# A graph layer and an expert layer on one core: all experts for eight node groups computed while edge rows are gathered, rows kept in DRAM, one-hot as stationary operand

## The chip, the cores and the metric

The kernel runs on one core of a Trainium2 chip. The metric is the device time of one launch in microseconds (us), the median of several runs.

## What is computed

12500 nodes have a row of 256 float32 each. There are two residual blocks, a graph layer and a mixture of experts:

```
x = x + segment_sum((layernorm(x) @ W)[src] * edge_weight[:, None], dst) + b      # 200000 edges
y = layernorm(x)
logits = mean(y, nodes) @ Wr + br            # one routing for all nodes
two experts of 8 are chosen, with weights r0 and r1
h_e = gelu(y @ W1[e] + b1[e]);  z_e = h_e @ W2[e] + b2[e]                          # 256 -> 512 -> 256
x = x + layernorm(y + r0 * z_e0 + r1 * z_e1) * gamma + beta
```

The edges come sorted by destination. The destination is `12500 * u**2` with uniform `u`, so that low nodes have far more edges than high ones: the first 128 nodes have about 158 blocks of 128 edges, the last 128 about 8. The routing depends on the mean over all nodes, so which two experts are needed is known only after the last node's first block is done.

## The kernel before

Nodes are cut into 98 tiles of 128 (`NT`), edges into 1563 blocks of 128 (`NE`). A small program (`Queue.put`, `Queue.run`) keeps a list of instructions for each engine, written in the order in which the source calls `put`; an instruction waits on the semaphores of its `after` list.

**Gather phase.** POOL (`gather`, L380) issues one indirect DMA for each edge block: 128 rows of `x` of 1 KB into `G`, a ring of 32 buffers. VectorE (DVE) takes the statistics of the gathered rows (`variance`, L395, `variance_end`, L401), works out the reciprocal roots for 8 blocks at a time (`power`, L412 to L427, written in between the other work), and builds a one-hot matrix scaled by weight and root (`one_hot`, L436, ring of 8). TensorE (PE) multiplies in `edge_tile` (L480): for each half of 128 columns of the block, `G` is the stationary operand and the one-hot moves, which adds to a 256 x 128 transposed sum in `ps` bank 0. Tiles are walked from node 0 up. When a tile's edges are through, `end_tile` adds the tile's column sum (L469), multiplies the sum by `W` (L473) and adds `b` (L474), then L487 begins the next tile with the edge block that straddles the border. ScalarE (ACT) takes the sum out (`node_tile`, L533), builds the one-hot of the straddling block, adds x, and computes mean and root (L543 to L560). All tiles of the new x stay in SBUF in `X`, 98 KB in each partition. All 12.8 MB of x are loaded into it by 25 DMAs at the start.

**Routing** is a chain of small instructions on PE, DVE and ACT (L624 to L665), then the two chosen experts are loaded and split in a high and a low part (L687, L688).

**Expert phase.** 25 groups of 4 tiles. `turn` (L591) transposes a normalised group on PE; `up` (L712) does 48 matmuls of 512 columns, `down` (L732) 96 of 256 columns, both in the high and low parts (three products), one pass of PE each. ACT computes the gelu twice (L716, L718), DVE the low part (`Hlo`, L721). The sum, the statistics and the normalisation of the group before are put between (`sum_up` L739 to L742, `rstd` L746 and L747, `finish` L752 to L757 with gamma and beta on POOL, `give` L763 and the store), as are `norm2` (L584), `rest_of_y` (L605) and `add_bias` (L611, POOL).

```
def edge_tile(r, gathered):
    ...
    for c in range(2):
        ins = e.matmul(ps[:, 0, c * P:(c + 1) * P], G[:, r, c * P:(c + 1) * P], OH[:, r % OHR, :], start=False, stop=True, skip_group_check=True)
    ins.then_inc(s_main.handle, 1)
    with e.While(lambda: e.snap(nxt) == e.snap(edge)):
        end_tile()
```

Of the kernel before, what the change touches and what calls it, by code (L numbers as in the profile page):

```python
# [12 lines left out]
HID = 2 * F // P  # L13
RING, OHR, NB = 32, 8, 8
# [3 lines left out]

class Sem:

    def __init__(self, handle):
        self.handle, self.value = handle, 0

class Queue:

    def __init__(self, new_sem):
        self.new_sem, self.sems, self.lists = new_sem, {}, {}  # L30

    def sem(self, name):
        if name not in self.sems:
            self.sems[name] = Sem(self.new_sem(name))
        return self.sems[name]

    def put(self, engine, fn, after=(), inc=None, by=1):
        s = self.sem(inc) if inc else None
        self.lists.setdefault(engine, []).append((fn, tuple(after), s, by))
        if s is None:  # L40
            return None
        s.value += by
        return (s, s.value)

    def run(self, engine, eng):
        reached = {}
        for fn, after, s, by in self.lists.get(engine, []):
            for w, v in after:
                if reached.get(w, 0) < v:
                    eng.wait_ge(w.handle, v)  # L50
                    reached[w] = v
            ins = fn(eng)
            if s is not None:
                ins.then_inc(s.handle, by)

def gnn_ffn(nc, x, dflat, srct, dstt, wt, W, b, Wr, br, W1, b1t, W2, b2, gamma, beta, cst, iota_e, out):
# [6 lines left out]

    srct_s, dstt_s, wt_s = dram("srct_s", (P, NE), i32), dram("dstt_s", (P, NE), i32), dram("wt_s", (P, NE))

    ctx = ExitStack()
    with ctx:
        def sb(name, shape, dt=f32):
            return ctx.enter_context(nc.sbuf_tensor(name, shape, dt))  # L70

        ctx.enter_context(nc.allow_non_contiguous_dma(reason="an expert's biases, an edge's columns"))
        q = Queue(lambda name: ctx.enter_context(nc.semaphore(name)))
        put = q.put

        X = sb("X", [P, NT, D])
# [5 lines left out]
        eps, half3, mhalf = sb("eps", [P, 1]), sb("half3", [P, 1]), sb("mhalf", [P, 4])  # L83
# [4 lines left out]

        base = (nc.sbuf_base + 31) // 32 * 32  # L90
        ARENA = 24576
        sb("arena", [P, ARENA + 8])

        class At:
# [778 lines left out]
```

## Time and profile before

| | us |
|---|---|
| median of 3 runs (2610.92 to 2613.72) | 2611.01 |
| span of the profiled execution | 2609.0 |
| first gather issued, last gather issued | 11.1, 1972.4 |
| last edge block on PE | 1985.1 |
| first matmul of the expert phase | 2006.4 |
| mean granted TensorE clock, share of full | 0.807 |

The span runs from the first instruction of an execution to its last. Engines run side by side and wait for each other by semaphores, so a share of busy time tells little by itself: the table shows two phases after each other, and each has to be read by what its own waits end on. The profiled execution's own time is its span and the few microseconds around it: 2609.0 against a median of 2611.0.

### The profile page before, as it was taken

What the parts mean: (1) busy time and instruction counts of PE and PEld (TensorE: products, weight loads), DVE (VectorE), ACT (ScalarE), POOL (GpSimd) and SP (SyncE); (2) the same over time, 40 slices, a digit from 0 to 9 for tenths busy, and PEclk for the clock granted to TensorE, in tenths of its full rate; (3) what the DMA queues carried; (4) which work ended last, traced back from release to release, by engine and by line L of the source; (5) the groups of instructions that cost most, each with busy time, mean ns of one, the idle gap of its engine ahead of it and who ended that gap; (6) DMA issues with size and microseconds to landing.
All of it is one profiled execution on the core that took longest, in us unless ns stands there. A gap on an engine that the chain in (4) does not pass through costs nothing.

```text
span 2609.0 us, 43640 instructions
## 1 busy us (share of the span) xinstructions
PE 2236.6 (86%) x11252; PEld 1768.6 (68%) x11253; DVE 1934.6 (74%) x8411; ACT 809.6 (31%) x2323; POOL 1725.3 (66%) x1665
## 2 busy tenths in 40 slices
PE   4799988888888888878788888888888999999998
PEld 3576666666666665665566655565666888888887
DVE  6777777777777777777777777777786666666666
ACT  0001000011121222223333344444456445444543
POOL 6777777777777777777777777777772343344344
PEclk9755566666667677778877898889898999999999
DMA  7633333333333333333333333333332000000000
GB/s 252 205 105 105 105 105 105 105 105 105 105 105 105 105 105 105 105 105 105 105 105 105 105 105 105 105 105 105 104 105 67 17 23 19 25 25 17 25 25 28
DMA packets 104845, 239.16 MB, mean 92 GB/s; under 512 B 26637, under 2 KB 53430, under 8 KB 104696
## 3 DMA queue, kind: packets, MB, share of 16 engines
q0 software_dynamic: 75024, 204.97, 26.9%
q1 hardware_dynamic: 29240, 30.25, 3.6%
q10 hardware_dynamic: 432, 2.40, 0.3%
q8 instruction: 40, 0.66, 0.1%
q14 instruction: 109, 0.89, 0.1%
HBM read 224.71 MB, written 12.80 MB: 91 GB/s over the span
## 4 chain that ended last, share of the span: by engine, by line
PE 43%; DMA 18%; POOL 17%; DVE 12%; issue 9%; ACT 1%; ACTq 0%; DVEq 0%; POOLq 0%
PE ps L480 19%; DMA G<-in_x,SRC 17%; POOL G L380 14%; PE ps L712 7%; PE ps L473 5%; PE ps L732 5%; PE ps L474 2%; PE ps L469 2%; DVE ST L395 2%; PE ps L487 2%; DVE OH L436 2%; POOL Z L755 1%; DVE Z L763 1%; DVE YTl L605 1%; DVE Hlo L721 1%
## 5 line engine op out<-in xcount | busy, mean ns | idle before, releaser
L380 POOL DMA_INDIRECT G<-in_x,SRC x1563 | 1486.4, 951 | 486.5 <-issue 292.5
L480 PE MATMUL ps<-OH,G 128*128 128x128 f32 x6252 | 1283.4, 356 | 310.1 <-DVE OH L436 292.6
L480 PEld LDWEIGHTS ps<-OH,G 128*128 128x128 f32 x6252 | 1041.2, 244 | 540.2 <-DVE OH L436 528.8
L395 DVE BATCH_NORM_STATS2 ST<-G 128x6 f32<-128x256 f32 x1563 | 666.6, 426 | 410.1 <-DMA G<-in_x,SRC 380.6
L436 DVE TENSOR_SCALAR OH<-CST,DL,WR 128x128 f32<-128x128 f32 x1563 | 530.8, 340 | 0.0
L533 ACT ACTIVATE AT<-ps 128x256 f32<-128x256 f32 x98 | 37.5, 383 | 1119.8 <-PE ps L480 1119.6
L401 DVE BATCH_NORM_AGGREGATE MV<-ST 128x2 f32<-128x6 f32 x1563 | 296.9, 190 | 6.8
L716 ACT ACTIVATE Ht<-ps,b1s 128x512 f32<-128x512 f32 (+1 forms) x200 | 136.4, 682 | 309.7 <-PE ps L712 292.4
L732 PE MATMUL ps<-W2h,Hhi 128*128 128x256 f32 x784 | 224.1, 286 | 0.4 <-DVE Hlo L721 0.4
L732 PE MATMUL ps<-W2l,Hhi 128*128 128x256 f32 x784 | 222.0, 283 | 0.0
L732 PE MATMUL ps<-W2h,Hlo 128*128 128x256 f32 x784 | 221.9, 283 | 0.0
L747 POOL TENSOR_TENSOR ZR<-ZR,mhalf 128x4 f32<-128x4 f32 (+1 forms) x25 | 26.3, 1053 | 290.2 <-DVE ZR L746 290.1
L721 DVE TENSOR_TENSOR Hlo<-Ht,Hhi 128x512 fp32r<-128x512 f32 (+1 forms) x200 | 129.7, 681 | 78.7 <-ACT Hhi L718 78.5
L763 DVE SCALAR_TENSOR_TENSOR Z<-X,NM,Z 128x256 f32<-128x256 f32 x98 | 89.1, 967 | 110.8 <-POOL Z L757 110.7
L473 PE MATMUL ps<-Wsb,AT 128*128 128x256 f32 x392 | 154.3, 532 | 3.2 <-ACT AT L533 1.9
L732 PEld LDWEIGHTS ps<-W2h,Hhi 128*128 128x128 f32 x784 | 150.5, 192 | 0.8 <-DVE Hlo L721 0.6
L732 PEld LDWEIGHTS ps<-W2l,Hhi 128*128 128x128 f32 x784 | 150.6, 192 | 0.0
L732 PEld LDWEIGHTS ps<-W2h,Hlo 128*128 128x128 f32 x784 | 150.5, 192 | 0.0
L473 PEld LDWEIGHTS ps<-Wsb,AT 128*128 128x128 f32 x392 | 92.5, 262 | 84.3 <-issue 72.6
L712 PE MATMUL ps<-YTh,W1h 128*128 128x512 f32 (+1 forms) x400 | 124.6, 393 | 13.5 <-DVE YTl L605 13.5
L718 ACT ACTIVATE Hhi<-ps,b1s 128x512 fp32r<-128x512 f32 (+1 forms) x200 | 135.1, 676 | 0.0
L755 POOL TENSOR_TENSOR Z<-Z,g_bc 128x1024 f32<-128x1024 f32 x24 | 95.3, 3973 | 58.2 <-DVE Z L752 58.2
(141 smaller groups left out, 2290.2 us busy)
## 6 DMA issues: line engine op xcount, KB each, us to landing
G<-in_x,SRC POOLq DMA_INDIRECT x1563, 2.7
X<-in_x SPq DMA_DIRECT2D x24, 512.0 KB
out<-Z SPq DMA_DIRECT2D x24, 512.0 KB, 3.0
W1s<-in_W SPq DMA_DIRECT2D x2, 512.0 KB, 4.4
W2s<-in_W SPq DMA_DIRECT2D x2, 512.0 KB, 6.1
DF<-in_dflat SPq DMA_DIRECT2D x1, 782.0 KB, 6.5
DST<-in_dstt ACTq DMA_DIRECT2D x1, 781.5 KB, 6.3
SRC<-in_srct ACTq DMA_DIRECT2D x1, 781.5 KB, 8.6
```

The lines of the kernel that those rows point to most:

```text
L380: gathered[s] = put("pool", lambda e: e.indirect_dma_start(out=G[:, s % RING, :], out_offset=None, in_=x, in_offset=bass.IndirectOffsetOnA ...
L395: bn[s] = put("dve", lambda e: e.bn_stats(ST[:, s % 4, :], G[:, s % RING, :]), after=[gathered[s]] + ([aggr[s - 4]] if s >= 4 else []), in ...
L401: aggr[s] = put("dve", lambda e: e.bn_aggr(MV[:, b_ % 2, k, :], ST[:, s % 4, :]), after=[bn[s]] + ([scaled[b_ - 2]] if b_ >= 2 else []), i ...
L436: oh[s] = put("dve", lambda e: e.tensor_scalar(OH[:, s % OHR, :], iota, DL[:, s:s + 1], WR[:, s + 1:s + 2], ALU.is_equal, ALU.mult), after ...
L473: e.matmul(ps[:, 1, 0:D], AT[:, c * P:(c + 1) * P], Wsb[:, c, :], start=False, stop=True, skip_group_check=True)
L480: ins = e.matmul(ps[:, 0, c * P:(c + 1) * P], G[:, r, c * P:(c + 1) * P], OH[:, r % OHR, :], start=False, stop=True, skip_group_check=True)
L712: hid[(g, i)] = put("pe", lambda e, c=c, k=k, f=f, bank=bank, wp=wp, yp=yp, st=(wp is W1h and yp is YTh and c == 0), en=(wp is W1l and c = ...
L716: h = put("act", lambda e, i=i, bank=bank, b1c=b1c: e.activation(Ht[:, i % HB, 0:n], ps[:, bank, 0:n], ACT.Gelu, bias=b1c), after=[hid[(g, ...
L718: h = put("act", lambda e, i=i, bank=bank, b1c=b1c: e.activation(Hhi[:, i, 0:n], ps[:, bank, 0:n], ACT.Gelu, bias=b1c), after=[w1_ok[1]] + ...
L721: hlo[(g, i)] = put("dve", lambda e, i=i: e.tensor_tensor(out=Hlo[:, i, 0:n], in0=Ht[:, i % HB, 0:n], in1=Hhi[:, i, 0:n].bitcast(f32), op= ...
L732: l2[(g, i)] = put("pe", lambda e, j=j, rows=rows, i=i, k=k, f=f, hp=hp, wp=wp, st=(i == 0 and j % 2 == 0 and hp is Hhi and wp is W2h), en ...
L755: gm = put(engine, lambda e: e.tensor_tensor(out=Z[:, g % 2, 0:n, :], in0=Z[:, g % 2, 0:n, :], in1=g_bc[:, :].unsqueeze(1).to_broadcast([P ...
```

## The change

The kernel is written anew as one program for each engine, with explicit waits. What it does otherwise:

- **Edges.** Edges and tiles are walked from the last node down. The one-hot is the stationary operand and `G` moves with 256 columns: one float32 product instead of two. The sum comes out as nodes x 256, so that a tile's end (a *section*) first transposes it. `G` has 64 buffers, `OH` 10; a gather waits for PE (`s_main`) and also for the statistics 32 blocks back (`s_bn`).
- **Sections** (`chores`) are spread over later ones: copy, transpose, product with `W` and `b`, x added, roots of a group of 4 tiles at a time, normalised rows transposed. Results go to DRAM: `x1_d` (the new x), `yt_d` (its normalised transpose). x is loaded tile by tile.
- **Units.** For the first 8 groups walked (`AHEAD`; the 32 tiles with the highest nodes), each of the 8 experts is computed in plain float32 while the gather goes on: 64 units. An up half is 8 products of 512 columns and four gelus, a down half 16 products of 256 columns and two copies; each unit loads 512 KB of `W1` and of `W2` and stores 512 KB to `y_d`. `events()` lists when each half is due; PE reads the due edge from a table (`EVT`) and branches.
- **After the routing** only 17 groups go through `up` and `down`. For the other 8 the two chosen experts' results are read back from `y_d`; they are put between the others (`order`, `pre_of`). Groups are not turned on PE, but read back transposed. POOL adds the second biases and `beta` (`add_rows`), DVE does all of the rest.

```diff
-RING, OHR, NB = 32, 8, 8
+RING, GS, OHR = 64, 32, 10
+AHEAD = 8
+UNITS = AHEAD * E
...
+def events():
+    free, u, out = 0.0, 0, []
+    for t in range(NT):
+        lo, hi = (min(NT - 1 - t + k, NODES / P) / (NODES / P) for k in range(2))
+        free += NE * (hi ** 0.5 - lo ** 0.5) * 0.8 - 2.9 if t >= 11 else 0.0
+        n = max(0, min(int(free / 14.2), UNITS - u))
+        n = UNITS - u if t == NT - 1 else n
+        free -= 14.2 * n
+        mine = [(round(64 * (k + 1) / (2 * n + 1)) / 64, kind, u + k // 2) for k, kind in enumerate([UPS, DOWNS] * n)]
...
-            for c in range(2):
-                ins = e.matmul(ps[:, 0, c * P:(c + 1) * P], G[:, r, c * P:(c + 1) * P], OH[:, r % OHR, :], start=False, stop=True, skip_group_check=True)
+            def edge(a, r):
+                g = e.snap(((a + r) & (RING - 1)) * D)
+                e.wait_ge(s_oh, a + (r + 1))
+                e.matmul(ps[:, 0, 0:D], OH[:, r, :], Gf[:, bass.ds(g, D)], start=False, stop=True, skip_group_check=True).then_inc(s_main, 1)
...
+            for s in range(NE):
+                if s >= RING:
+                    e.wait_ge(s_main, s - RING + 2)
+                if s >= GS:
+                    e.wait_ge(s_bn, s - GS + 1)
+                e.indirect_dma_start(out=G[:, s % RING, :], out_offset=None, in_=x,
...
+            def chores(v):
+                e.wait_ge(s_as, v + 1)
+                e.wait_ge(s_at, v + 1)
+                for c in range(2):
+                    ins = e.transpose(ps[:, TA, c * P:(c + 1) * P], AS[:, c * P:(c + 1) * P], ident)
+                ins.then_inc(s_ta, 1)
+                e.wait_ge(s_pre, v + 1)
+                for c in range(2):
+                    e.matmul(ps[:, XB, 0:D], AT[:, c * P:(c + 1) * P], Wsb[:, c, :], start=False, stop=True, skip_group_check=True)
+                e.matmul(ps[:, XB, 0:D], ones[0:1, :], b_row[0:1, :], start=False, stop=True, skip_group_check=True).then_inc(s_w, 1)
...
+            def unit_up(u):
+                e.wait_ge(w1_in, u * 16 + 16)
...
+                for i in range(4):
+                    e.wait_ge(s_gelu, u4 + (i + 1))
+                    for c in range(2):
+                        ins = e.matmul(ps[:, UP[i % 2], :], W1u[:, c, i * P:(i + 1) * P], YU[:, c, :], start=(c == 0), stop=(c == 1))
+                    ins.then_inc(s_up, 1)
...
+            def unit_down(u):
...
+                for p in range(2):
+                    e.wait_ge(s_ye, u * 2 + (p + 1))
+                    for h in range(2):
+                        j = 3 - (2 * p + h)
+                        for i in range(4):
+                            ins = e.matmul(ps[:, DN[p], h * D:(h + 1) * D], H[:, i, j * P:(j + 1) * P], W2u[:, i, :],
+                                           start=(h == 0 and i == 0), stop=(i == 3), skip_group_check=True)
+                    ins.then_inc(s_dn, 1)
...
+            with e.Fori(0, NE // OHR) as i:
+                a = e.snap(i * OHR)
+                e.reg_mov(rel, e.snap(due) - a)
+                for half in (range(0, OHR // 2), range(OHR // 2, OHR)):
+                    with e.If(e.snap(rel) > half[-1]):
+                        for r in half:
+                            edge(a, r)
+                    with e.If(e.snap(rel) <= half[-1]):
+                        for r in half:
+                            event(a, r, edge(a, r))
...
+                    else:
+                        e.wait_ge(yp_in[g % 2], 32 * (g // 2 + 1))
+                        e.scalar_tensor_tensor(out=Z[:, n % 2, q, :], in0=YP[:, g % 2, 0, q, :], scalar=r1[:, 13:14], in1=XN[:, n % 3, q, :], op0=ALU.mult, op1=ALU.add).then_inc(s_zy, 1)
...
+                        e.scalar_tensor_tensor(out=Z[:, n % 2, q, :], in0=YP[:, g % 2, 1, q, :], scalar=r1[:, 14:15], in1=Z[:, n % 2, q, :], op0=ALU.mult, op1=ALU.add).then_inc(s_z, 1)
```

## Rows read from the trace of the kernel before

**Rows 1.** The page's first lines: span, then busy time and share of each engine.

```profile
span 2609.0 us, 43640 instructions
PE 2236.6 (86%) x11252; PEld 1768.6 (68%) x11253; DVE 1934.6 (74%) x8411; ACT 809.6 (31%) x2323; POOL 1725.3 (66%) x1665
```

**Rows 2.** Stretches: window, length, busy us (instructions), granted clock, DMA share, GB/s.

```profile
60.00:100.00 40.00, 27.87 (x130) 23.37 (x128) 29.32 (x153) 0.00 (x0) 30.43 (x32) 0.74 0.76 231
200.00:400.00 200.00, 178.09 (x675) 136.57 (x674) 155.75 (x759) 17.43 (x58) 151.42 (x160) 0.60 0.36 105
1600.00:1900.00 300.00, 250.77 (x1274) 181.98 (x1272) 232.25 (x1136) 140.00 (x494) 227.18 (x240) 0.86 0.36 105
2300.00:2600.00 300.00, 290.41 (x1902) 265.17 (x1900) 199.48 (x450) 137.31 (x230) 123.35 (x51) 1.00 0.07 22
```

**Rows 3.** Instructions in order of time: POOL's gathers without and with a wait.

```profile
12.58 0.95 POOL L380 DMA_INDIRECT G<-in_x,SRC  x1 [0.30 <-issue]
...
1972.41 0.94 POOL L380 DMA_INDIRECT G<-in_x,SRC  x1 [0.30 <-PE ps L480]
```

**Rows 4.** Waits: us in total, times, longest.

```profile
DVE ST L395 <- DMA G<-in_x,SRC: 380.6, 1141, 2.2
...
PEld ps L487 <- issue: 38.9, 97, 0.7
```

**Rows 5.** In order of time, PE: a tile's end and the burst after it.

```profile
692.54 0.79 PE L469 MATMUL ps<-X,RCOL 128*1 x2
693.25 1.13 PE L473 MATMUL ps<-Wsb,AT 128*128 128x256 f32 x4
694.32 0.69 PE L474 MATMUL ps<-b_row,ones 1*128 1x256 f32 x2
694.94 0.71 PE L487 MATMUL ps<-OHX,G 128*128 x4
...
1952.01 4.35 PE L480 MATMUL ps<-OH,G 128*128 128x128 f32 x32
```

**Rows 6.** The chain that ended last, two groups of the expert phase: start, us, what.

```profile
2019.48 11.54 PE ps L732 x96
2031.02 10.91 PE ps L712 x48
...
2296.51 11.15 PE ps L712 x48
...
2320.68 11.15 PE ps L712 x48
```

**Rows 7.** PE alone in two windows; columns as in Rows 2 without the other engines.

```profile
304.00:308.00 4.00, 3.55 (x13) 0.50 0.37 108
320.00:324.00 4.00, 4.00 (x24) 0.89 0.36 102
```

**Rows 8.** Around the routing, in order of time.

```profile
1985.13 0.52 PEld L480 LDWEIGHTS ps<-OH,G 128*128 128x128 f32 x4 [0.18 <-issue]
...
1992.49 1.28 ACT L623 ACT_TABLE_LOAD   x1
...
2006.41 1.20 PE L712 MATMUL ps<-YTh,W1h 128*128 128x512 f32 x2
```

**Rows 9.** DMA issues: KB each, median us from issue to landing.

```profile
W1s<-in_W SPq DMA_DIRECT2D x2, 512.0 KB, 4.4
```

**Rows 10.** Groups of instructions (busy us, mean ns) in the window from 2200 to 2500 us.

```profile
L716 ACT ACTIVATE Ht<-ps,b1s 128x512 f32<-128x512 f32 x103 | 71.1, 690 | 169.6 <-PE ps L712 161.1
...
L741 DVE BATCH_NORM_STATS2 ZST<-Z 128x6 f32<-128x256 f32 x52 | 22.2, 428 | 1.8
...
L584 DVE TENSOR_SCALAR Y<-X,R 128x256 f32<-128x256 f32 x52 | 14.8, 349 | 0.0
```

**Rows 11.** Single lines: durations in ns, min/median/max, of all of the span.

```profile
L763 DVE SCALAR_TENSOR_TENSOR Z<-X,NM,Z x98: 471/474/2628, 2049.8 to 2604.7; 128x256 f32<-128x256 f32 x98
L611 POOLq MODIFY_POOL_CONFIG  x2: 33/35/37, 1973.3 to 1973.4; - x2
```

More of the change, by code:

```diff
@@ L12 @@
 NC = (NE + P - 1) // P
-HID = 2 * F // P
-RING, OHR, NB = 32, 8, 8
+RING, GS, OHR = 64, 32, 10
+SHIFT = (NT - 1) * P
 LN_EPS = 1e-5
 CAPACITY = float(-(-NODES * 5 // (4 * E)))
[L19 to L54, printed above, removed]
@@ L57, in gnn_ffn, with tiles, slot, sections @@
-def gnn_ffn(nc, x, dflat, srct, dstt, wt, W, b, Wr, br, W1, b1t, W2, b2, gamma, beta, cst, iota_e, out):
+GT = 4
+NG = (NT + GT - 1) // GT
+AHEAD = 8
+UNITS = AHEAD * E
+HID = 2 * F // P
+HB = 4
+VIRTUAL = 4
+FINAL = NT - 1 + VIRTUAL
+END, EXTRA, UPS, DOWNS = range(4)
+def tiles(g):
+    return range(g * GT, min((g + 1) * GT, NT))
+def slot(t):
+    return len(tiles(t // GT)) - 1 - t % GT
+def sections():
+    copied = [v if v < NT - 1 else NT - 1 if v == FINAL else None for v in range(FINAL + 5)]
+    out, waiting, turned = [], [], None
+    for v in range(FINAL + 5):
+        x1 = copied[v - 2] if v >= 2 else None
+        root = x1 // GT if x1 is not None and (x1 == NT - 1 or x1 % GT == GT - 1) else None
+        waiting += tiles(root) if root is not None else []
+        xh = waiting.pop(0) if waiting else None
+        out.append({"copy": copied[v], "across": copied[v - 1] if v else None, "x1": x1, "root": root, "xh": xh, "yt": turned})
+        turned = xh
+    assert not waiting and turned is None
+    return out
@@ L190, in gnn_ffn @@
[L190 to L198 removed]
+        OHX, OHT = early("OHX", [P, P]), early("OHT", [P, 2, P])
@@ L726, in down @@
-        def down(g):
-            for i in range(HID):
-                k, f = i // 4, i % 4
-                for j, t in enumerate(tiles(g)):
-                    rows = slice(j * P, (j + 1) * P)
-                    for hp, wp in ((Hhi, W2h), (Hhi, W2l), (Hlo, W2h)):
-                        l2[(g, i)] = put("pe", lambda e, j=j, rows=rows, i=i, k=k, f=f, hp=hp, wp=wp, st=(i == 0 and j % 2 == 0 and hp is Hhi and wp is W2h), en=(i == HID - 1 and hp is Hlo): e.matmul(
-                            ps[:, j // 2, j % 2 * D:(j % 2 + 1) * D], hp[:, i, rows], wp[:, k, f, :], start=st, stop=en, skip_group_check=True),
-                            after=[hlo[(g, i)], w2_ok[k]] + ([z[(g - 1, j // 2 * 2 + 1)]] if g else []), inc="pe_down")
-                    l2[(g, "end", j)] = l2[(g, i)]
@@ L843 @@
+            up(0)
+            for k in range(len(post)):
+                down(k)
+                if k + 1 < len(post):
+                    up(k + 1)
 def kernel(**inputs):
@@ L859 @@
     cst[0, 5 * P + E] = 1 << 20
+    evt = np.zeros((NT + 1, 2 * NEV), np.float32)
+    for n, (t, c, kind, _) in enumerate(EVENTS):
+        evt[t, 2 * n] = 1 - c
+        evt[t + 1, 2 * n] = c if t + 1 < NT else c * (NE - 1)
+        evt[NT, 2 * n + 1] = kind
+    evt[NT, 2 * NEV - 2] = 1 << 20
     arrays = {
```

1422 lines of the change are left out of this document (877 added, 545 removed).

## The prediction

> **What bounds the kernel now.** The busy table comes first [rows 1]: TensorE 86%, DVE 74%, POOL 66%, none of them full. Cut into stretches [rows 2] it falls into two phases. Between 200 and 400 us POOL starts 160 gathers, 1.25 us each, and it does the same in every stretch until its last one; from 2300 on it does something else. In order of time [rows 3] the first gathers, which wait for nothing, and the last, which wait for PE, show the same picture: about 0.95 us of work and 0.30 us until the next. (1972.41 - 12.58) / 1561 gathers is 1.255 us. So in the gather phase nobody but POOL sets the pace: PE and DVE wait for it, DVE 380.6 us for the gathers' data [rows 4]. That PE is 89% busy from 200 to 400 us [rows 2] is no contradiction. Its granted clock is 0.60 there: PE was let run mostly at 1.2 GHz, because what it has to do fills a slow PE and would leave a fast one half empty. In the burst after a late tile's end 32 matmuls of 128 columns take 4.35 us at full clock [rows 5], 0.136 each, four to an edge block: 0.54 us of work in 1.255.
>
> In the expert phase the chain of what ended last [rows 6] is made of PE's `up` and `down`: 11.15 and 11.54 us, and one group takes 2320.68 - 2296.51 = 24.17 us. PE is 97% busy at full clock there [rows 2]. The kernel is thus 1974 us of POOL, 32 us of tail and routing, 603 us of PE. The change moves PE work out of the third part into the idle half of PE in the first.
>
> **PE's prices in the new gather phase.** From [rows 6], one-pass matmuls of 512 columns cost 10.91 / 48 = 0.227 us, of 256 columns 11.54 / 96 = 0.120: 0.42 ns a column and pass and 13 ns an instruction. A float32 product runs as two instructions (L480's x32 in [rows 5] are 8 blocks of 2 products), each of two passes. So 256 columns cost 2 x (512 x 0.42 + 13) = 0.456 us, 512 columns 0.886. The tile's end gives the upper bound: L473's two products of 256 columns take 1.07 us from start to start, 0.535 each, with a gap in it [rows 5]. I take 0.47 for 256 columns, near the steady stream, and 0.89 for 512.
>
> - Edge: 0.47 us (0.456 to 0.535), against 0.54 now.
> - Section: from L469's start to the next burst is 695.49 - 692.54 = 2.95 us now (L487 starts at 694.94, 0.55 before the burst) [rows 5]. L469 goes (0.71), four transposes come (4 x 0.13 by the burst's price, 0.5), the rest stays: 2.75, with two waits for ACT that aren't in it now. I take 2.9, bounds 2.75 and 3.8 (one further idle 0.4 us as before each L487, 38.9 / 97 [rows 4], at each of its two transposes).
> - Unit: 8 x 0.89 + 16 x 0.47 = 14.6 us (14.4 to 16).
>
> By the destination's density the first 11 tiles take 87 blocks; until then no unit is scheduled and PE follows POOL: 11 + 87 x 1.255 + 10 for DVE's lead = 130 us. What follows is 1476 x 0.47 = 694, 91 sections x 2.9 = 264, 64 units x 14.6 = 934: 1892 us, and PE is through at 130 + 1892 = 2022. POOL alone would let it finish where it does now, at 1985 [rows 8]. **So the new bound of the gather phase is PE, not POOL, by a small margin**, and the last edge moves by +37 us. Both ends: 1985 (edge 0.456, section 2.75, unit 14.4 give 1976, less than POOL) and 130 + 1476 x 0.535 + 91 x 3.8 + 64 x 16 = 2290. Of the clock: the level stayed at 1.2 GHz in a window in which PE waited for a one-hot now and then, and 2.4 GHz came in one in which it had fallen behind and had its work waiting (4.00 us of 4 busy, 0.89) [rows 7]. The new schedule leaves PE hardly a gap, so I count 2.4 GHz throughout, and put slow starts into the bounds.
>
> **What I cost at nothing there, and its cover.** POOL's second wait: the first one cost nothing [rows 3]; bounds 0 and 0.035 us, the nearest small item in POOL's queue [rows 11], x 1499 = 52 us, of which the 37 us that PE is late hide most. Loads and stores of the units: 1.5 MB each, 98 MB over some 1850 us, 53 GB/s on top of 105. From 60 to 100 us the chip moves 231 GB/s with gathers still at 1.25 us [rows 2]; landing is later, but 64 buffers stand in for it. Behind a wait of SP's queue stand the next unit's weights: single buffers, 4.4 us to land [rows 9], with half a unit (7 us of PE) in between: hidden while units are spread, 2 us exposed if they touch. The whole load of x at the start goes. ACT: 140 us of 300 in the last third, with a tile every 18 us [rows 2]; units bring four gelus of 0.69 us [rows 10] and two copies no longer than these per 25 us and a table load of 1.28 us [rows 8] when gelu and root alternate. It stays below two thirds; a late gelu makes PE wait only past its second bank (1.8 us). DVE's work per edge is unchanged; it is held by `OH` at 10 blocks, more than a half unit's 6.
>
> **Tail to the expert phase.** Now 2006.41 - 1985.13 = 21.3 us [rows 8]. Instead of one section five follow the last edge, about 2.6 us each of hops between ACT and PE, of which the old end had 7 us already: +6. Before the first exponential ACT has two new jobs in its queue, `high(0)` and `normal2(0)`; the second waits for the first group's x1, which SP loads only after the last row's store has landed: store and load at some 4 us each [rows 9] and 4 activations, less what the route needs until then, +5. Mean and sum are shorter: -3. So 29 us (25 to 40): the first `up` at 2022 + 29 = 2051.
>
> **Expert phase.** Now 2609.0 - 2006.4 = 602.6 us. A group without its turn costs PE 11.1 + 11.5 = 22.6 us; the first takes 24.6 as now (2031.02 - 2006.41). 17 groups remain, the last with 2 tiles. DVE must keep up: now 199.48 / 300 x 24.17 = 16.1 us a group [rows 2], of which about 2.15 is L763 standing still (2.628 against a median of 0.474) behind a POOL operation [rows 11]: 13.9. Eight operations of some 0.35 [rows 10] go, four of 0.474 come: 13.9 - 2.8 + 1.9 = 13.0. A group read back from DRAM adds 16 operations of 0.474, four of 0.43 [rows 10] and small ones: 9.9. So a window with such a group costs DVE 22.9 us, and PE has 22.6. With a standstill of 2.15 us behind each of POOL's two long operations a group, 17.3 and 31.5. I take 25 us for each of the 7 full windows with such a group (22.6 to 31), since each is followed by one with slack; `Hlo` is late then, and PE waits in `down`. Sum: 24.6 + 8 x 22.6 + 7 x 25 + 20 for the last window (half of PE's work, all of DVE's) + 10 for the last output (12 now, with POOL in it) = 410 (395 to 450).
>
> **Sum.** 2051 + 410 = 2461 us of span; the profiled execution lies 2.0 below the median, so 2463 us, 5.7% faster.
>
> **Rivals.**
> 1. *PE keeps pace*, and POOL stays the bound: every price at its lower end, last edge at 1990, first `up` at 2018, 400 after it: 2420. For it: the stream prices of [rows 6] are of this very length. Against it: 64 starts of halves and 91 sections must then cost no bubble at all.
> 2. *PE falls well behind*: waits for ACT at sections, cold starts and late weights cost 1 to 2 us for each of some 155 sections and units beyond my prices. Last edge 2080 to 2180, total 2520 to 2600. For it: there is no slack left, so each bubble goes straight to the end. Against it: a late PE has its work waiting for it, and runs at full clock.
> 3. *Slower than before*: PE's sequencer. Each edge now has a computed address and wait, and where an event is near a test and a branch; if this doesn't fit under 0.47 us of matmul, it counts at all 1476 edges. It decides from (2609 - 2461) / 1476 = 0.10 us per edge; at 0.15 the time is 2685. Against it: in the burst [rows 5] the edge loop with its test keeps 0.136 us per matmul, nearly the one-pass price of 2 x 128 x 0.42 + 13 = 0.12, so that no more than 0.07 us per edge can be control. For it: the cover shrinks from 0.54 to 0.47, and the loop body holds code of units that is jumped over. The Trainium skill (Advanced Engine Details and Errata, "Control Flow Timing") gives about 108 ns for a compare-and-branch; if one were exposed at each edge, the estimate would be 159 us more, 2622. That rule speaks against the change; the burst, where a test per edge is hidden, against its bare use.
> 4. *The second phase gives little*: DVE bounds it, 31 us in each window with a group read back: 7 x 6 more, 2505. It joins any of the others and widens the range.
>
> **Chances.** Forecast (2440 to 2510) 0.45; rival 1 (below 2440) 0.2; rival 2 (2510 to 2605, rival 4 in it) 0.25; rival 3 0.08; within 0.2%, about what a measurement of this kernel can tell from none, 0.02. Faster 0.9, same 0.02, slower 0.08. The range leaves out rival 3 and little at either end: 2405 to 2590.
>
> **What would show it.** Right: gathers at more than 1.26 us apart for long stretches of the second half with waits on PE; a granted clock above 0.95 there; PE above 90% busy; L480's successor at 0.47 us in a burst; last edge near 2022; 22.6 us between `up`s without, some 25 with a group read back; 17 groups' work after the routing. Wrong: gaps in PE's stream at each edge in a backlog (rival 3), a granted clock below 0.9 (rival 2), gathers at 1.255 to the end (rival 1), or PE waiting for `Hlo` in every window (rival 4). The prediction fails most easily in the unit and the section, since 1 us more in each is 155 us of 148 that are gained.

## The result

The changed kernel takes 4145.7 us (median of 4, 4137.3 to 4168.4) where the kernel before takes 2611.0: a ratio of 1.589 (95% interval 1.584 to 1.593). Forecast were 2463 us, 2405 to 2590. It is slower by 1535 us, and the forecast was 1683 us too low.

From the page of the changed kernel, profiled execution: span and busy shares, the clock by slices, the queue that brings TensorE's instructions (packets, MB), and three of the costliest groups (busy us and mean ns; idle time before them and its main cause).

```profile
span 4146.8 us, 54848 instructions
PE 2911.7 (70%) x9926; PEld 1916.8 (46%) x9927; DVE 1792.0 (43%) x8271; ACT 1089.6 (26%) x2904; POOL 1640.6 (40%) x1642
PEclk8788888777778777777777787878888889898898
q8 instruction: 606, 9.93, 1.1%
L447 POOL DMA_INDIRECT G<-in_x,SRC x1563 | 1483.8, 949 | 2025.2 <-DVE ST L810 1274.2
L1096 PE MATMUL ps<-G,OH 128*128 x3120 | 1102.5, 486 | 1002.5 <-issue 834.2
L825 DVE TENSOR_SCALAR OH<-CST,DL,WR 128x128 f32<-128x128 f32 x1563 | 556.6, 356 | 2094.2 <-PE ps L1096 2080.9
```

Against [rows 1] every engine is less busy, TensorE with 70% instead of 86. POOL now waits mostly for DVE's statistics, and DVE for the edge product (2080.9 us), so PE holds the chain of the gather. Yet PE stands idle ahead of that product, 834.2 us of it for "issue": the profile shows nothing that it waited for. And `q8` moved 9.93 MB in packets of 16 KB (it is TensorE's: in the two runs below that lengthen TensorE's program alone, only it grows). Before it was

```profile
q8 instruction: 40, 0.66, 0.1%
```

The reading, which the experiments test, is that the loop's code is fetched again and again. PE in order of time (start, duration, count, idle time before):

```profile
2011.27 2.07 PE L1096 MATMUL ps<-G,OH 128*128 x4 [11.75 <-issue]
...
2015.00 0.64 PE L1049 MATMUL ps<-CST,AS 128*128 128x128 f32 x2
...
2023.28 7.77 PE L1096 MATMUL ps<-G,OH 128*128 x26 [2.90 <-issue]
...
2043.94 4.38 PE L1096 MATMUL ps<-G,OH 128*128 x10 [4.65 <-issue]
2048.63 0.69 PE L1096 MATMUL ps<-G,OH 128*128 x2 [0.30 <-DVE OH L825]
2049.86 7.13 PE L1073 MATMUL ps<-YU,W1u 128*128 128x512 f32 x16 [0.54 <-issue]
```

Half a unit of 8 products of 512 columns takes 7.13 us, as forecast (8 x 0.89). The edge products right behind a gap are slower: two edges in 2.07 us, thirteen in 7.77 (0.60 each, forecast 0.47). The time lies in gaps of 3 to 12 us.
```profile
L1117 PEldq COMPARE_BRANCH  x1: 7344/7344/7344, 2000.1 to 2000.1; - x1
L1121 PEldq COMPARE_BRANCH  x1: 2899/2899/2899, 2007.7 to 2007.7; - x1
```

They fill 10.2 us of it. Summed over the trace's records, 304 of the 3070 branches in PE's program last over 1 us, 957 us together; in the kernel before not one of 1806 does (the longest 0.56 us). Of the 188 gaps over 1 us that are put down to issue in the gather, 821 us, 170 hold such a branch.

The last edge starts at 3577.3 instead of 2022, the first `up` (L1153) at 3617.3, and from there to the end it is 529.5 us instead of 410. So of the 1686 us that the span exceeds the forecast of 2461, the gather accounts for 1555, the tail for 11, the expert phase for 119.

### The profile page after: what moved, and what is told of

The parts are those of the page before. It is cut to its first block and busy times, and to the rows that moved or that the text cites. A ratio compares the mean times of both kernels' runs of the same rounds, so it can differ in the third digit from the quotient of the medians.

```text
span 4146.8 us, 54848 instructions
## 1 busy us (share of the span) xinstructions
PE 2911.7 (70%) x9926; PEld 1916.8 (46%) x9927; DVE 1792.0 (43%) x8271; ACT 1089.6 (26%) x2904; POOL 1640.6 (40%) x1642
## 3 DMA queue, kind: packets, MB, share of 16 engines
q8 instruction: 606, 9.93, 1.1%
## 5 line engine op out<-in xcount | busy, mean ns | idle before, releaser
L447 POOL DMA_INDIRECT G<-in_x,SRC x1563 | 1483.8, 949 | 2025.2 <-DVE ST L810 1274.2
L1096 PE MATMUL ps<-G,OH 128*128 x3120 | 1102.5, 486 | 1002.5 <-issue 834.2
L825 DVE TENSOR_SCALAR OH<-CST,DL,WR 128x128 f32<-128x128 f32 x1563 | 556.6, 356 | 2094.2 <-PE ps L1096 2080.9
L1096 PEld LDWEIGHTS ps<-G,OH 128*128 128x128 f32 x3120 | 656.1, 232 | 1427.5 <-issue 1358.6
L1084 PE MATMUL ps<-W2u,H 128*128 128x256 f32 x2048 | 530.9, 424 | 54.1 <-issue 54.1
L1073 PE MATMUL ps<-YU,W1u 128*128 128x512 f32 x1024 | 520.4, 666 | 27.2 <-issue 22.1
L1084 PEld LDWEIGHTS ps<-W2u,H 128*128 128x128 f32 x2048 | 435.3, 216 | 159.8 <-issue 89.5
L628 ACT ACTIVATE H<-ps,b1a 128x512 f32<-128x512 f32 x256 | 175.6, 687 | 702.7 <-PE ps L1073 702.7
L1073 PEld LDWEIGHTS ps<-YU,W1u 128*128 128x128 f32 x1024 | 213.9, 215 | 314.9 <-issue 307.6
L635 ACT ACTIVATE YE<-ps 128x512 f32<-128x512 f32 x128 | 76.4, 597 | 1008.7 <-PE ps L1084 1008.7
L1178 PE MATMUL ps<-W2l,Hhi 128*128 128x256 f32 x528 | 164.4, 311 | 0.0
L1178 PE MATMUL ps<-W2h,Hlo 128*128 128x256 f32 x528 | 164.2, 311 | 0.0
```

Source lines behind the costliest of these rows:

```text
L447: e.indirect_dma_start(out=G[:, s % RING, :], out_offset=None, in_=x, in_offset=bass.IndirectOffsetOnAxis(ap=SRC[:, s:s + 1], axis=0)).the ...
L628: e.activation(H[:, i, :], ps[:, UP[i % 2], :], ACT.Gelu, bias=b1a[:, u % E, i:i + 1]).then_inc(s_gelu, 1)
L825: e.tensor_scalar(OH[:, s % OHR, :], iota, DL[:, s:s + 1], WR[:, s + 1:s + 2], ALU.is_equal, ALU.mult).then_inc(s_oh, 1)
L1073: ins = e.matmul(ps[:, UP[i % 2], :], W1u[:, c, i * P:(i + 1) * P], YU[:, c, :], start=(c == 0), stop=(c == 1))
L1084: ins = e.matmul(ps[:, DN[p], h * D:(h + 1) * D], H[:, i, j * P:(j + 1) * P], W2u[:, i, :], start=(h == 0 and i == 0), stop=(i == 3), skip ...
L1096: e.matmul(ps[:, 0, 0:D], OH[:, r, :], Gf[:, bass.ds(g, D)], start=False, stop=True, skip_group_check=True).then_inc(s_main, 1)
```

## The experiments

The kernel before does not take the same time everywhere: 2611 us on the first chip and on one other, 3100 to 3121 us on four more. I call these two kinds of chip. Each verdict goes against the kernel before on its own chip, and sums are made within one kind.

The expectations weigh four theories. A: code that doesn't stay with the sequencer is fetched again. B: branches, waits and computed addresses cost time at each edge, whatever the length. C: the ring of one-hots is too short. D: code that is jumped over costs time by its length, even when it isn't fetched again.

**Fetching again.** Ring and loop body shortened from 10 slots to 8 and to 6:

```diff
-RING, GS, OHR = 64, 32, 10
+RING, GS, OHR = 64, 32, 8
```

> The changed kernel with OHR 8 in place of 10: the ring of one-hots and with it TensorE's loop body are a fifth shorter (by a count of the program some 85 KB of instructions at 64 bytes against 107; the kernel before has some 92 KB). Nothing else changes. Theory A (instruction fetch: the body of 107 KB no longer stays where TensorE's sequencer keeps it and is fetched again in each pass): the instruction queue's 9.93 MB fall to about 1 MB, the idle time of TensorE put down to issue all but goes, gathers come every 1.25 to 1.3 us, the last edge at about 2030 us, total 2570 to 2620. Theory B (computed addresses, waits and branches cost time at each edge whatever the body's length): 4050 to 4200, since the same number of each is executed. Theory C (the ring is what TensorE and DVE wait on): slower than 4146, as the ring is shorter.

> The same with OHR 6: a body of some 64 KB, a ring of 6 one-hots. Theory A: as with OHR 8, 2570 to 2650, a little slower than it where DVE now waits for the shorter ring during a half unit of 7 us. Theory B: 4050 to 4200. Theory C: slower than with 8.

Bodies of 85 and 64 KB instead of 107: 3624.4 us against 3105.9, 1.167 (1.162 to 1.172), and 3673.7 us, 1.184 (1.179 to 1.189). 33 and 26 instruction packets: nothing is fetched again. Neither A alone (2570 to 2620, or some 490 more on this kind of chip) nor B alone (4050 to 4200) comes out, and C, slower than before, falls. To have the changed kernel itself on such a chip, three runs side by side:

> The kernel before, unchanged, profiled anew. On the chip of the last four runs it took 3106 us and not 2611. If this chip is like the first: 2611, gathers 1.255 us apart. If it is like the second: about 3106, and its trace shows gaps of TensorE put down to issue in its loop over the edges, which the first chip's trace hasn't, while its instruction queue moves the same 0.66 MB (theory B: time at branches and waits without a fetch) or several MB (theory A: fetches).

> The changed kernel, unchanged, on the same chip, for comparison: 4146 if the chip is like the first; on the other, theory A says about as much or more, theory B (a slower sequencer) clearly more than 4146.

> The changed kernel with OHR 8 again, on a chip whose before and after are known too. The last time its instruction queue moved 0.54 MB, so the refetching was gone, and it still took 3624. Theory A on a chip like the first: 2570 to 2620, since the refetching was all. Theory B on it: 3400 or more, since branches cost time beside it.

Before 3120.9, changed 4457.0 (one time each), body of 8 slots 3605.6 (two). The product's idle time in the changed kernel and with 8 slots:

```profile
L1096 PE MATMUL ps<-G,OH x3120: 379/478/791, 66.6 to 3886.8; 128*128 x195
its engine sat idle before it (us, times) until:
  issue: 1010.4, 329
```
```profile
L1096 PE MATMUL ps<-G,OH x3120: 379/379/791, 66.7 to 3035.4; 128*128 x195
its engine sat idle before it (us, times) until:
  issue: 482.1, 279
```

The last edge comes 851 us earlier with 579 packets less, 1.5 us each. PE's branches say the same: 1426 us in all in the changed kernel, 300 of them over 1 us; 552 us and 4 with 8 slots. Half of the idle time for issue remains, and of the loss against the kernel before 485 of 1336 us. Is length enough by itself? The kernel before, with 1 or 12 matmuls that never run, behind the tile's end in the `While` of each edge:

```diff
+                    with e.If(e.snap(slot) < 0):
+                        for _ in range(12):
+                            e.matmul(ps[:, 2, 0:D], ones[:, :], zed, start=True, stop=True, skip_group_check=True)
```

> The kernel before with code that is never executed put in its loop over the edges: behind each tile's end one matmul under a condition that is always false, 32 copies, which brings the body from some 92 to some 104 KB. It computes the same. Theory A: if the limit lies between 92 and 104 KB, the instruction queue moves several MB more, gathers come at 1.5 to 2.3 us, total 3000 to 4100; if it lies above 104 KB, nothing. Theory B: 2611 plus or minus 5, since only some 98 tests more are executed.

> The same with 12 matmuls in each copy: a body of some 192 KB. Theory A: above any limit so far, so that most of the body is fetched in each of 48 passes: 6 to 10 MB more on the instruction queue, gathers well above 1.255 us apart, total 3000 to 4500. Theory B: 2611 plus or minus 5.

104 KB: 458 packets, 1.017 (1.011 to 1.023), which is not clear of 2%. 192 KB: 710 packets, 1.054 (1.047 to 1.060). Fetching again begins between 92 KB (before) and 101 KB (below), by my count of the code. The whole loses only 50 and 164 us by it, where theory A asked for 3000 us and far more on the faster kind. That is not because a fetch is cheap here: PE's branches take 1415 us with 192 KB, against 362 before on such a chip, 1053 us for 670 packets or 1.6 us each, as in the changed kernel ((1426 - 552) / 579 = 1.5). With 104 KB it is 752 us, 0.9 us a packet. But the last edge comes only 157 us later (2653.1 after 2495.7): PE had idle time here, under POOL's pace, and the fetches mostly fill it. And a longer body of the changed kernel, 12 slots and 128 KB:

> The changed kernel with a ring of 12 one-hot slots: body 128 KB instead of 107. Theory A (a refetched 16 KB costs 1.5 us: the changed kernel fetched 579 packets more than the body of 8 slots and took 850 us more; e8_skip32 gives 1.57): 130 passes of 8 packets are at most 1040 packets, so up to 640 us over the changed kernel's 4457 on this chip, 4800 to 5150 if nearly all is fetched in each pass. Rival (the changed kernel's loss is not from fetching): within 3% of 4457 or under.

761 packets, 4519.0 us against 2612.3, 1.726 (1.719 to 1.733). The changed kernel took 4145.7 on a chip of that kind: 373 us for 155 packets, 2.4 us each, of which 210 us, 1.4 each, are PE's branches (1662 after 1452). The direction is as expected, the count (up to 1040) is not; a pass need not touch all of the code, which no run counts.

**One copy of the event code.** My theory now was D, that the length walked and jumped over costs even without fetching. The code of sections and units stands once instead of ten times (19 KB of body); a pass over the slots does the edges up to the next event, and tests find the way back in:

```diff
-                for half in (range(0, OHR // 2), range(OHR // 2, OHR)):
-                    with e.If(e.snap(rel) > half[-1]):
-                        for r in half:
-                            edge(a, r)
-                    with e.If(e.snap(rel) <= half[-1]):
-                        for r in half:
-                            event(a, r, edge(a, r))
+                e.reg_mov(cur, 0)
+                with e.While(lambda: e.snap(cur) < OHR):
+                    for r in range(OHR):
+                        with e.If(e.snap(cur) == r):
+                            with e.If(e.snap(rel) >= r):
+                                edge(a, r)
+                                e.reg_mov(cur, r + 1)
+                    last = e.snap(e.snap(cur) - 1)
+                    event(a, last, e.snap(((a + last) & (RING - 1)) * D))
```

> The changed kernel with one single copy of the event code (sections and units) in TensorE's loop instead of ten: the body shrinks from 107 KB to 19 KB of instructions, and no large piece of code is jumped over between two edges. All work, the ring of 10 one-hot slots and the order of the work are as in the changed kernel; the control code per edge is somewhat more (a compare and branch for each slot in each pass, two to three passes for a block of ten). Theory A+D (the time is that of instruction supply: refetching, and a price for each 16 KB that a walk or a jump crosses): the gather falls back to near the sum of the unit prices, edge phase ended at 2000 to 2150, whole time 2550 to 2700 on a chip where the kernel before takes 2611; on a chip where it takes 3106, under 3250 and so at least 10% under the body of 8 slots (3624). Theory B (the computed addresses, waits and branches themselves): no gain over the body of 8 slots, ratio to the kernel before 1.16 or more, since the control work has grown.

> The kernel with one copy of the event code, and behind each of the ten slots 32 float32 matmuls (8 KB of instructions) under a condition that is never true: body 101 KB, little enough not to be refetched at 107 KB minus what the body of 8 slots showed. Against e9_skip1 (the same condition with 1 matmul) only the length of the code jumped over differs. Theory D (each 16 KB crossed costs 1 to 3 us even without refetching): about two and a half passes of 80 KB for each of 156 blocks are some 1900 crossings, so 500 us or more above e9_skip1. Rival (code that is resident costs nothing to jump over; only refetching and branches cost): within 50 us of e9_skip1.

> The kernel with one copy of the event code, and behind each of the ten slots one float32 matmul under a condition that is never true: body 24 KB. It adds ten compares and branches to each pass over the slots, some 2.5 passes for each of 156 blocks, about 3900 in all. Theory D: within 60 us of e6_shared, since branches over short code are hidden by the matmuls. Theory B (a branch costs 0.1 us on the path): 200 to 400 us above e6_shared.

One copy: 5347.2 us, 1.725 (1.720 to 1.731). My theory fell: the shortest body is far slower. Ten more tests a pass over one matmul each: 6365.3 us; over 32 each (body 101 KB): 9814.0 us. The first two move 24 packets of instructions, the third, which I had expected to stay in place, does not:

```profile
q8 instruction: 2227, 36.49, 1.7%
```

3640 tests more (the trace's count) cost 1018 us, 0.28 us each, far more than either theory had (within 60, or 200 to 400). The same tests over 8 KB cost 3449 us more, but with 2203 packets more, 1.6 us each. Length or fetching? The same over 4 KB, body 60 KB:

> As e8_skip32, with 16 instead of 32 float32 matmuls behind the condition that is never true: 4 KB jumped over each time instead of 8, body 60 KB, which is not refetched. Against e9_skip1 (0.25 KB jumped over, 6365) the branches are the same, 3570. Theory (length costs only by refetching; e8_skip32 fetched 2227 packets of 16 KB, 2203 more than e9_skip1, for 3450 us, 1.57 us for each): within 150 us of e9_skip1. Theory D (each 16 KB crossed costs 1 to 3 us): about 800 crossings more, 800 to 2400 us above it.

6184.1 us and 26 packets, on a chip where the kernel before takes 2612. The times can't be compared, the chips being of two kinds: it is 181 us faster than the 6365.3 with short jumps, and if the whole 490 us between the kinds were taken off those, it would be 310 us slower, still far from the 800 to 2400 that theory D asked for. The branches themselves can. The tests over one matmul, over 4 KB and over 8 KB (ns, min/median/max):

```profile
L1128 PEldq COMPARE_BRANCH  x3640: 1/208/1099, 66.9 to 5785.9; - x192
L1128 PEldq COMPARE_BRANCH  x3640: 208/208/358, 49.2 to 5609.0; - x192
L1128 PEldq COMPARE_BRANCH  x3640: 3/215/2948, 67.1 to 9281.4; - x192
```

A jump over 4 KB that stay in place takes 0.208 us, as over one matmul; all branches of the program take 1758 and 1773 us, and 5386 us where the code is fetched again. Jumping over code costs nothing more that shows; fetching it again costs.

**No control at all.** PE's gather loop as a straight line for this input: constants for waits and addresses, the edges at which sections and units are due as a list. The kernel before likewise. Then one and four tests behind each edge of the straight line (one edit stands here for three):

```diff
+            for s in range(NE):
+                g = s % RING * D
+                e.wait_ge(s_oh, s + 1)
+                e.matmul(ps[:, 0, 0:D], OH[:, s % OHR, :], Gf[:, g:g + D], start=False, stop=True, skip_group_check=True).then_inc(s_main, 1)
+                with e.If(e.snap(never) != 0):   # 0, 1 or 4 of these
+                    e.matmul(ps[:, XB, 0:D], ones[:, :], zed, start=False, stop=True, skip_group_check=True)
+                while at < len(EVENTS) and DUE[at] == s:
+                    ...
```

> The changed kernel with TensorE's gather loop written out as one straight line for this input: no branch, no computed address, no wait against a register, no reading of the event table; the edges at which sections and units are due stand in the code as a list. Each of its matmuls and constant waits is issued in the same order as in the changed kernel. About 1 MB of instructions, each fetched once. Theory B (branches and the register work around them set the pace: walking through the control flow of each kernel with this input gives 4470 branches and 29.7 thousand instructions for the body of 8 slots, 10,000 and 43.5 for the one copy, 13,600 and 50.6 for the one copy with ten more tests a pass; from 3036 to 4779 to 5786 us of gather, 0.28 us for a branch with its register move): the gather ends at 2000 to 2200, and the whole comes to 2550 to 2750, under the kernel before (3106) by 11% or more even where that takes 3106. Theory D (each 16 KB crossed costs 1 to 3 us): some 70 crossings against 1290, so the same time within 200 us. Theory A (fetching from DRAM is what costs): 1 MB to fetch against 9.9 MB, 65 packets of 16 KB; if the fetch is not ahead of the engine, up to 2.6 us each, 170 us more. Rival (the work itself, other than the unit prices say, holds the engine): the gather still ends after 2700.

> The kernel before with TensorE's gather loop written out as one straight line for this input in the same way (1563 edges, 98 ends of tiles, constants for every wait and address). Walking through the control flow of the kernel before gives 3310 branches and 23.5 thousand instructions. Theory B: its 470 us of TensorE's idle time put down to issue go, and the gather is then held by GpSimd's descriptors: 300 to 600 us faster than 3106. Rival (its branches are hidden, as I took them to be): within 2% of the kernel before.

> The straight line of e10_straight with one register move, one compare-and-branch (always taken, over a single matmul) behind each of the 1563 edges. Theory B with 0.28 us each and nothing hidden: 440 us above e10_straight. With the 0.45 us of matmuls of an edge as cover, where the sequencer runs ahead: under 60 us. Between them, the share that is hidden.

> The straight line of e10_straight with four register moves and compare-and-branches (each taken, over one matmul) behind every edge, instead of the one of e13_branch, which cost nothing. Theory (TensorE's sequencer needs 0.28 us for a branch with its move, as the ten more tests a pass showed, and this is hidden as long as it is less than the 0.45 us of an edge's matmuls): 4 x 0.28 = 1.12 us, 0.67 more than an edge's matmuls, for 1563 edges at most 1050 us above e10_straight (3219), and 600 to 1050 with part of it under the sections and units. Rival (a branch ahead in straight code costs nothing, only jumps inside a loop do): within 60 us. A second price in it: 4 MB of instructions, 250 packets of 16 KB read once, against 80.

Straight: 3219.6 us against 3105.1, 1.038 (1.031 to 1.046), with 80 packets; the last edge at 2652 instead of 3035 with 8 slots. Without control 386 us go, but not the 850 and more that I had expected (2550 to 2750 us); what holds the rest is taken up below. The kernel before gains nothing from it, 1.007 (1.004 to 1.010): its control was hidden, the rival was right. One test an edge: 1.038 (1.035 to 1.041), nothing again. Four tests, on a chip of the 2612 kind: 3740.0, 1.431 (1.429 to 1.434). That is 520 us above the straight line, under the 600 to 1050 expected, but the straight line itself ran only on the slower kind and may take less here. PE there, in order of time:

```profile
1514.91 1.22 PE L1097 MATMUL ps<-G,OH 128*128 128x256 f32 x2 [0.81 <-DVE OH L828]
1516.36 1.22 PE L1097 MATMUL ps<-G,OH 128*128 128x256 f32 x2 [0.23 <-issue]
...
1528.05 1.22 PE L1097 MATMUL ps<-G,OH 128*128 128x256 f32 x2 [0.26 <-issue]
1529.50 0.80 PE L1097 MATMUL ps<-G,OH 128*128 128x256 f32 x1 [0.23 <-issue]
```

Ten edges in 1529.50 - 1514.91 = 14.59 us, 1.46 an edge: 0.36 us for each test with its register move (and its matmul that isn't run). In the sequencer's records one test starts 0.35 us after the other, 0.20 us of it the branch itself:

```profile
L1099 PEldq COMPARE_BRANCH  x6252: 200/200/367, 49.1 to 3169.4; - x196
```

One of them fits under an edge's 0.46 us of product, four don't. PE runs at the lower clock in this stream (granted 0.53 of full speed from 1514 to 1530 us), 1.22 us for the two instructions of a product, which take 0.69 elsewhere; even so each product ends before the next is issued.

So the price has a threshold, somewhere between one test and four. PE's branches as the traces record them (all, for each edge, and how many of them last over 1 us, with their sum), beside loop size, packets and last edge:

```
kernel            branches  per edge   over 1 us (us)    KB   packets  last edge, us
before              1806      1.2          0             92      40    2496
straight line          1      0            0              -      80    2652
  one test          1564      1.0          0              -     117    2633
body of 8 slots     3105      2.0          4 (11)        86      27    3035
changed             3070      2.0        300 (916)      107     606    3887
one copy            7698      4.9          2 (3)         19      24    4779
  ten more tests   11338      7.3          2 (4)         24      24    5786
  over 8 KB        11338      7.3       1356 (3686)     101    2227    9282
```

(All on chips where the kernel before takes 3100 to 3121.)

**The expert phase.** With five instead of three buffers for the X1 rows read back, in the one copy and in the straight line:

```diff
-                if n + 3 < NG:
-                    load_x1(n + 3)
+                if n + 5 < NG:
+                    load_x1(n + 5)
```

> The kernel with one copy of the event code, and five instead of three buffers for the reloaded X1 rows in the expert phase (the reload of group n+5 is issued where that of n+3 was). Theory (ScalarE's in-order queue stands still at the normalisation of a group for the reload of its X1 rows, and GELU behind it with it): the time from the first up matmul of the expert phase to the end falls from 530 to 410 to 450 us, the whole time by 80 to 110 us against the kernel with three buffers. Rival (the windows are held by the units of VectorE and ScalarE themselves, the wait for the reload only shows where slack lies): under 20 us gained, and the pair of windows stays at 62 us.

> The straight line with five instead of three buffers for the reloaded X1 rows. Against e10_straight, the wait of ScalarE for the reload of X1 goes, by what the one copy with five buffers gained over the one copy with three (72 us): 50 to 100 us less. Rival (VectorE and ScalarE themselves hold the windows): what was gained there is all there is, and the expert phase stays over 450 us instead of 410.

72 us less in both: 5275.7 after 5347.2 (80 to 110 less were expected), and 3148.0 after 3219.6. ACT in the changed kernel (order of time) and the waits of the straight line's expert phase, first with three buffers, then with five (us in total, times, longest):

```profile
3844.85 0.68 ACT L709 ACTIVATE Ht<-ps,b1s 128x512 f32<-128x512 f32 x1
3845.42 0.69 ACT L712 ACTIVATE Hhi<-ps,b1s 128x512 fp32r<-128x512 f32 x1
3859.28 2.07 ACT L673 ACTIVATE XN<-XL,NR,R 128x256 f32<-128x256 f32 x4 [13.18 <-DMA XL<-x_d]
3861.26 0.67 ACT L709 ACTIVATE Ht<-ps,b1s 128x512 f32<-128x512 f32 x1
```
```profile
DVE Hlo L929 <- ACT Hhi L715: 152.2, 31, 8.6
ACT XN L676 <- DMA XL<-x_d: 152.2, 15, 14.4
...
PE ps L1152 <- DVE Hlo L929: 99.3, 33, 6.0
```
```profile
DVE Hlo L929 <- ACT Hhi L715: 60.6, 20, 8.2
...
PE ps L1152 <- DVE Hlo L929: 45.6, 26, 3.8
```

ACT stands still 13 us in the middle of a group's gelus for rows that SP loads only after it has issued an earlier group's output; DVE's `Hlo` and PE's `down` are late behind it. With five buffers the wait is gone and the phase takes 3141.4 - 2685.3 = 456 us instead of 531. The straight line with it is still 1.015 (1.011 to 1.020) of the kernel before, on a chip where that takes 3105. None of the kernels run beats the kernel before. Where that takes 2611, the straight line was not run.

## Why the prediction was wrong

**What held.** "The new bound of the gather phase is PE": the waits say so. The prices of the work: half a unit 7.13 us (8 x 0.89); an edge in a full stream 0.46, six in 2.75 us in the second of these rows of the one-test line (forecast 0.47):

```profile
1515.74 0.64 PE L1052 MATMUL ps<-CST,AS 128*128 128x128 f32 x2
...
1519.21 2.75 PE L1097 MATMUL ps<-G,OH 128*128 128x256 f32 x12
```

The section just before runs from 1515.74 to 1519.21, 3.5 us (forecast 2.9, bounds 2.75 to 3.8). The traffic of the units never came to matter: PE never waited for their weights. POOL's second wait held it for 1274.2 us, but behind DVE and PE, which were late.

**The step that failed** is rival 3's dismissal: "no more than 0.07 us per edge can be control", 0.08 of the chances. It decided at 0.10 us an edge. The burst [rows 5] showed PE's products back to back with a test at each edge, and I read that as control costing next to nothing. It shows only that control is *shorter than the cover*. What it costs stood in the trace of before, where I had not looked, in the records of PE's sequencer (ns); an edge has 0.54 us of products over it:

```profile
L482 PEldq COMPARE_BRANCH  x1757: 75/207/562, 45.0 to 1985.3; - x196
```

Before, an edge has 1.2 branches. The changed loop has 2.0, unevenly: a half of five edges without an event has only the two of the half, the others have a test at each edge, and each event a reload of its table entry. Two branches at 0.35 us are 0.7 us an edge, an estimate from the four-test line, and the cover had shrunk to 0.47. The reload alone (ns) is 229 x 0.54 = 123 us, where before 97 loads took 0.30 each:

```profile
L1114 PEldq TENSOR_LOAD <-EVT x229: 532/539/774, 60.1 to 3570.9; - x115
```

What counts is the length of the sequencer's work beside that of the engine's, and the burst only bounded it from above, by 0.54. The Trainium skill (Advanced Engine Details and Errata, "Control Flow Timing") has some 108 ns for a compare-and-branch and 51 for a jump; the runs show 0.20 us for one that jumps, 0.07 for the shortest, and 0.28 to 0.36 for a test with all that goes with it, about three times as much, and none of it where it is covered.

**What was missing altogether** is the fetching. I named "the loop body holds code of units that is jumped over" and gave it no price; no row of before could, since its 92 KB stay in place (40 packets). The 107 KB do not: 606 packets, and 957 us in branches of over 1 us on the first chip. The Trainium skill (the same page, "ISA Cache") gives TensorE 128 KB in lines of 16 KB. The line agrees with the trace (9.93 MB in 606 packets); the size doesn't serve as a limit here, as fetching begins between 92 and 101 KB.

**Sizes.** Where the kernel before takes 3105 us, the parts add up: of the changed kernel's 4457, fetching is 851 (4457 to 3606), control with the reload of events 386 (to 3220), the X1 reload 72 (to 3148), and 43 are left. On the first chip those runs were not made, but its trace splits the 1555 us of the gather (window, length, busy us of PE and the others, clock):

```profile
130.00:3577.00 3447.00, 2395.56 (x7239) 1474.92 (x7239) 1349.40 (x7185) 826.59 (x2402) 1393.48 (x1470) 0.80 0.33 100
```

PE should have been busy for 1892 us without a gap. It was idle for 1051 us, 895 of them for issue, and busy for 504 us more than forecast, at a granted clock of 0.80 and with many products standing alone (0.69 us instead of 0.46). How the idle time divides between fetching and the rest of control there is shown only by the 957 us in long branches, part of which lies under PE's work.

The straight line's last edge lies 156 us behind that of before (2652 to 2496), where I had forecast 37. Part of it are waits of PE for ACT within units and sections, which I had at nothing beyond the second bank:

```profile
PE ps L1076 <- ACT H L631: 142.1, 33, 9.4
PE ps L1067 <- ACT AS L522: 121.6, 33, 9.7
```

In the changed kernel on the first chip PE waited for ACT's gelus 4.9 us in all; but it was late itself there, so what the waits would be without gaps is open, the more as on the other kind of chip ACT stands idle for issue too, 73.9 us of it ahead of its gelus. **Rival 2** is thus right in its sign, a clock below 0.9, and in part in its cause, by a size that I can't give for the first chip. Whether the change would win there without fetching and control is not shown.

**Granted clock.** "It leaves PE hardly a gap, so I count 2.4 GHz throughout" fell with the gaps: 0.75 to 0.79 from 800 to 2800 us, against 0.88 to 0.91 in the straight line from 800 to 2400 us. **Tail**: 40 instead of 29 us, at the top of its range. **Expert phase**: 529.5 instead of 410. I priced the reload of x1 once, before the first group, and not in the steady state, where a ring of three makes ACT's in-order queue wait for it in each window with a group read back. With five buffers it is 456, six us above the range's end of 450; the rest I have not traced.

## What to carry to other kernels

Before work is moved into a loop, count for one turn what the sequencer must do (compares, jumps, register work) and set it beside the engine time that covers it: below it is free, above it every turn pays. A burst without gaps shows that control is hidden, not what it costs; the sequencer's own records, under the line of the loop or the test, do show it. Count the loop's code in KB too, all copies of unrolled bodies together, and look at the packets of the instruction queue: a queue that moves more than the program's size says that the loop doesn't stay. And of a reload through a ring, ask which in-order queue waits for it in the steady state.

## What was not expected of the hardware

- A test in TensorE's program costs nothing at one an edge and 0.36 us at four an edge. The branch itself is recorded with 0.20 us where it jumps.
- Fetching again costs 1.5 to 1.6 us of TensorE's sequencer for 16 KB in most pairs of runs (0.9 and 1.4 in two), as the branches' records have it. How much the kernel loses by it depends on the cover: 164 us of 1053 in the kernel before with 192 KB, nearly all in the one copy over 8 KB (3449 us of time for 3613 us more in branches).
- Jumping over 4 KB that stay in place takes as long as jumping over one matmul, 0.208 us.
- The same program takes 2611 us on some chips and 3100 to 3121 on others. The expert phase is the same there, 602.9 us (before 602.6), and so are the products; the gather is not. PE waits at regular places in the unchanged loop though nothing is fetched again (221.6 us for issue ahead of the edge product), while on the first chip the same product waited 0.2 us in all for issue. DVE's one-hot and POOL's gather stand still in these places too, 494.7 and 247.3 us put down to a remote cause. The straight line lessens PE's gaps (131.7 us) and doesn't remove them. Where they come from is open, and so is whether the chip itself is the cause: no run changed only that.

```profile
604.11 4.61 PE L480 MATMUL ps<-OH,G 128*128 128x128 f32 x20 [2.90 <-issue]
...
612.98 6.16 PE L480 MATMUL ps<-OH,G 128*128 128x128 f32 x28 [2.86 <-issue]
...
623.26 1.22 PE L480 MATMUL ps<-OH,G 128*128 128x128 f32 x4 [2.87 <-issue]
```
